# The second query halves turned on VectorE, and two large transfers moved in the first turn

## The reference

```python
q = (x @ Wq.T)                      # 32 heads of 128
q = q * cos + rotate_half(q) * sin  # rotate_half: [-q2, q1], halves of 64
k, v = low-rank keys (part of them rotated too), values   # 8 key/value heads
scores = q @ k.T / sqrt(128), causal; attn = softmax(scores)
x = layernorm(x + (attn @ v) @ Wo.T)
x = layernorm(x + W2(silu(W1 x) * (W3 x)))   # 4-bit weights
```

## Time and profile before

| What | Before |
|---|---|
| median of three runs | 2376.82 us |
| the profiled execution, its span | 2375.78 us, 2374.0 us |
| TensorE matmul busy | 2359.8 us, 99% of the span |
| ScalarE busy | 1619.1 us, 68% |
| VectorE busy | 1425.0 us, 60% |
| GpSimd busy | 577.5 us, 24% |
| chain that ended last | TensorE 96%, DMA 2%, ScalarE 1%, VectorE 1% |
| `b_ys<-y_d`, a load of 256 KB, to landing | 2.7 us |

### The profile page before, as it was taken

The page is one execution under the profiler, slowest core; times in us unless marked ns, Lnnn a source line. Parts: engine busy times, 40 slices in busy tenths (PEclk is TensorE's granted clock), DMA queues, the critical chain, the costliest instruction groups (busy, mean ns, idle before and its releaser), DMA issues.

```text
span 2374.0 us, 40892 instructions
## 1 busy us (share of the span) xinstructions
PE 2359.8 (99%) x11999; PEld 1994.7 (84%) x11999; DVE 1425.0 (60%) x3797; ACT 1619.1 (68%) x3223; POOL 577.5 (24%) x451
## 2 busy tenths in 40 slices
PE   9999999999999999999999999999999999999998
PEld 8888888888888888888888888888888888888887
DVE  5335667676766676666666676767676675243333
ACT  4224878888888888887878888888888885222221
POOL 3102323333232323232323333232323220000000
PEclk9999999999999999999999999999999999999999
DMA  6778534435354444344434445354434435320110
GB/s 224 263 259 276 173 133 143 146 129 166 116 173 126 159 134 145 128 141 150 137 131 138 147 135 173 107 176 131 155 126 145 132 138 199 131 72 36 53 36 18
DMA packets 133256, 338.42 MB, mean 143 GB/s; under 512 B 13344, under 2 KB 30752, under 8 KB 122656
## 3 DMA queue, kind: packets, MB, share of 16 engines
q1 hardware_dynamic: 133200, 337.70, 42.1%
HBM read 230.17 MB, written 109.84 MB: 143 GB/s over the span
## 4 chain that ended last, share of the span: by engine, by line
PE 96%; DMA 2%; ACT 1%; DVE 1%; issue 0%; POOL 0%; SPq 0%; ACTq 0%; DVEq 0%; POOLq 0%
PE b_ps L269 45%; PE b_sps L269 32%; PE b_tps L1658 10%; PE b_tps L1717 3%; PE b_ps L1717 3%; PE b_tps L269 2%; DMA v_d<-a_vs 1%; DMA b_kt<-k_d 0%; DMA b_wraw<-in_wqT 0%; ACT b_sc L1102 0%; ACT b_sc L1108 0%; PE b_tps L1579 0%; PE b_sps L1667 0%; ACT b_pt L1123 0%; DVE b_sc L1330 0%
## 5 line engine op out<-in xcount | busy, mean ns | idle before, releaser
L1348 DVE TENSOR_TENSOR b_pt<-b_tps,b_pt 128x512 fp32r<-128x512 f32 (+3 forms) x768 | 426.4, 555 | 304.5 <-ACT b_pt L1123 300.3
L269 PE MATMUL b_sps<-b_kt,b_qs 128*128 128x512 f32 (+4 forms) x2304 | 496.8, 343 | 1.5 <-DMA b_kt<-k_d 1.1
L1108 ACT ACTIVATE b_sc<-b_sc,b_rinv 128x896 f32<-128x896 f32 (+7 forms) x512 | 396.0, 774 | 105.1 <-DVE b_rinv L1338 98.2
L269 PEld LDWEIGHTS b_sps<-b_kt,b_qs 128*128 128x128 f32 x2304 | 403.5, 188 | 55.9 <-issue 2.5
L1123 ACT ACTIVATE b_pt<-b_tps 128x512 fp32r<-128x512 f32 (+3 forms) x768 | 367.4, 478 | 117.3 <-PE b_tps L1658 115.8
L269 PE MATMUL b_ps<-b_pt,b_vt 128*128 128x512 f32 x1584 | 423.9, 399 | 0.3 <-DVE b_ys L1359 0.3
L1102 ACT ACTIVATE b_sc<-b_sc,b_nmax 128x896 f32<-128x896 f32 (+7 forms) x512 | 395.4, 772 | 38.3 <-DVE b_nmax L1330 34.8
L269 PE MATMUL b_ps<-b_xs,b_wq 128*128 128x512 f32 x1512 | 418.7, 402 | 0.0
L269 PE MATMUL b_ps<-b_wo,b_ot 128*128 128x512 f32 x1536 | 415.6, 403 | 0.0
L1330 DVE CUSTOM_DVE_ANT_0 b_sc<-b_sps,b_mask 128x896 f32<-128x896 f32 (+7 forms) x512 | 386.2, 754 | 18.2 <-PE b_sps L269 18.0
L1658 PE MATMUL b_tps<-b_ident,b_sc 128*128 128x128 f32 x2304 | 349.9, 273 | 4.5 <-ACT b_sc L1108 2.3
(11 more groups left out here) (183 smaller groups left out, 2260.2 us busy)
## 6 DMA issues: line engine op xcount, KB each, us to landing
b_xs<-xs_d SPq DMA_DIRECT2D x32, 2048.0 KB, 9.2
y_d<-b_ys SPq DMA_DIRECT2D x128, 256.0 KB, 3.0
b_ys<-y_d SPq DMA_DIRECT2D x121, 256.0 KB, 2.7
b_wraw<-in_wqT SPq DMA_DIRECT2D x64, 256.0 KB, 2.7
k_d<-a_ks SPq DMA_DIRECT2D x32, 512.0 KB, 4.1
v_d<-a_vs SPq DMA_DIRECT2D x32, 512.0 KB, 3.0
b_kt<-k_d SPq DMA_DIRECT2D x64, 256.0 KB, 4.6
b_vt<-v_d SPq DMA_DIRECT2D x16, 1024.0 KB, 4.8
```

Of the source, the lines that this page charges most:

```text
L269: ins = nc.tensor.matmul(out, *every[n], start=(n == 0), stop=(n == len(every) - 1))
L1108: nc.scalar.activation(sc[:, slot, 0:w], sc[:, slot, 0:w], ACT.Copy, scale=rinv[:, slot:slot + 1])\
L1348: nc.vector.tensor_tensor(pt[:, u, LO, 0:nj, h * P:(h + 1) * P], tps[n % 2][:, 0:nj], pt[:, u, HI, 0:nj, h * P:(h + 1) * P], ALU.subtract) ...
```

## The change

Four things are done.

1. For `q1` VectorE now multiplies the product bank by the sine table itself, in two instructions of 64 partitions that also swap the halves (`turn_q`), just ahead of the cosine multiplication. ScalarE's copies and GpSimd's multiplication of `q1` are gone; `q0` stays as it was.
2. For this the second half of the sine table is loaded with its partition halves swapped: three DMAs where there was one.
3. SP issues the 2 MB store `xs_d<-a_xe` (`a_store_x(END)`) ahead of END's first value store, and no longer in step 6 of the first turn. The copy `y_d<-in_x` of 2304 KB goes from step 13 to step 21 of the first turn.
4. The padding ahead of the loop is changed on ScalarE and VectorE.

```diff
--- before.py
+++ after.py
@@ -821,9 +821,7 @@
                         for p in range(4):
                             sp.wait_ge(a_v_out[p], 16 * (V_USES[p] if p >= 2 else 4) + a_OUT0)
                         load_v(0)
-                    if turn == "first" and step == 6:
-                        a_store_x(END)
-                    if turn == "first" and step == 13:
+                    if turn == "first" and step == 21:
                         sp.dma_start(y_rest, x_rest).then_inc(a_y_out, 16)
                     for _bk, kind, a, g in finished(step, turn, 1):
                         if kind == "q0" and a == 3:
@@ -869,11 +867,14 @@
                 sp.wait_ge(a_k_out[slot], 16 * 2 * 2)
             for n in range(8):
                 if n == 2:
-                    sp.dma_start(sinq[:], sinT).then_inc(tab_in, 16)
+                    sp.dma_start(sinq[:, 0:TB], sinT[:, 0:TB]).then_inc(tab_in, 16)
+                    for half in (0, 64):
+                        sp.dma_start(sinq[64 - half:128 - half, TB:S], sinT[half:half + 64, TB:S]).then_inc(tab_in, 16)
                     sp.dma_start(cosq[:], cosT).then_inc(tab_in, 16)
                 if n == 4:
                     load_k(0)
                 a_store_k(END, n)
+            a_store_x(END)
             for n in range(V_LATE):
                 a_store_v(END, n)
             sp.wait_ge(q_mm, 4)
@@ -962,8 +963,8 @@
                         if kind in ("q0", "q1"):
                             split_q(it + g, int(kind == "q1"), h)
                     for _bk, kind, h, g in finished(step, turn, 1):
-                        if kind in ("q0", "q1"):
-                            times_sin(it + g, int(kind == "q1"), h)
+                        if kind == "q0":
+                            times_sin(it + g, 0, h)
                     if turn != "end" and step in WO_SPLIT:
                         split_wo(it, WO_SPLIT.index(step))
                     if turn in ("first", "loop") and step in WQ_SPLIT:
@@ -980,7 +981,7 @@
             split_wq(0, 3)
             for t in range(2, NBLK):
                 a_rope_lo(t)
-            pool.wait_ge(tab_in, 32)
+            pool.wait_ge(tab_in, 64)
             for h in range(GQ):
                 times_sin(0, 0, h)
             turns(pool, turn_of)
@@ -1062,7 +1063,7 @@
                 a_nope_hi(t)
                 for n in range(8):
                     a_v_hi(t, n, a_bank[(VG + n) % a_RING])
-                    for _ in range(4 if n < 4 else 4):
+                    for _ in range(5 if n < 4 else 4):
                         act.sem_inc(placed, 1)
                 a_rope_hi(t + 1)
 
@@ -1130,8 +1131,8 @@
                 nc.scalar.activation(ot[:, i % 2, HI], banks[bk], ACT.Copy).then_inc(ot_hi, 1)
 
             def take(bk, kind, it, a):
-                if kind in ("q0", "q1"):
-                    swap_q(it, int(kind == "q1"), a, bk)
+                if kind == "q0":
+                    swap_q(it, 0, a, bk)
                 elif kind == "va":
                     a_v_hi(END, a, banks[bk])
                 elif kind == "pv":
@@ -1301,9 +1302,17 @@
                 a_nope_lo(t)
                 for n in range(8):
                     a_v_lo(t, n, a_bank[(VG + n) % a_RING])
-                    for _ in range(3 if n < 4 else 3):
+                    for _ in range(2):
                         dve.sem_inc(placed, 1)
                 a_rope(t + 1)
+
+            def turn_q(it, h, bk):
+
+                n = 8 * it + 4 + h
+                dve.wait_ge(q_mm, n + 1)
+                dve.wait_ge(add_done, n + 1)
+                nc.vector.tensor_tensor(sw[0:64], banks[bk][64:128], sinq[64:128, TB:S], ALU.mult).then_inc(sw_done, 2)
+                nc.vector.tensor_tensor(sw[64:128], banks[bk][0:64], sinq[0:64, TB:S], ALU.mult).then_inc(sin_done, 1)
 
             def cos_q(it, blk, h, bk):
                 n = 8 * it + 4 * blk + h
@@ -1359,6 +1368,8 @@
                 nc.vector.tensor_tensor(ys[:, i % 2], banks[bk], ys[:, i % 2], ALU.add).then_inc(y_added, 1)
 
             def take(bk, kind, it, a):
+                if kind == "q1":
+                    turn_q(it, a, bk)
                 if kind in ("q0", "q1"):
                     cos_q(it, int(kind == "q1"), a, bk)
                 elif kind == "va":
@@ -1536,10 +1547,12 @@
             for n in (2, 3):
                 for m in range(4):
                     a_made_lo(n, m)
+            for _ in range(3):
+                dve.sem_inc(placed, 1)
             for t in range(END):
                 a_block_of(t)
             a_nope_lo(END)
-            dve.wait_ge(tab_in, 32)
+            dve.wait_ge(tab_in, 64)
             dve.wait_ge(masked, 4)
             for h in range(GQ):
                 cos_q(0, 0, h, Q_BANK[h])
```

## The result

The changed kernel takes 2392.1 us, median of six runs (2389.8 to 2392.5), against 2377.2 for the kernel before in six runs, three of which are those of the table ahead of the prediction: ratio 1.0062, 95% interval 1.0051 to 1.0072. It is 15 us slower where 4 us of gain were forecast (2372.8 us, range 2369.6 to 2377.2). The profiled execution took 2392.5 us with a span of 2390.7.

What follows compares the result with a forecast made beforehand. TensorE was taken to bound the kernel, busy 99% of the span. Gains of 2.3 + 1.5 + 0.4 less 0.2 us for the first turn gave 4.0 us: 2376.8 to 2372.8 us, range 2369.6 to 2377.2.

Steps and rivals of the forecast that it cites:

- The 2 MB store and the copy of `y`: First turn: earlier store gains 3.8 us (bounds 0 and 3.8), copy at step 21 gains 0.4 (-0.5 to 0.8).
- stall, clock and the wait for weights: First turn, TensorE: 2.3 us stall near 239 us, 1.5 of lower clock behind it, 0.41 for late query weights, all to go.
- ScalarE and GpSimd lose the part, worth 0: Loop: 76 us less on ScalarE, 83 less on GpSimd; TensorE waits for neither, so gain 0 (bounds 0 and 1).
- VectorE gains it; "1.2 to 1.4 us a head": VectorE's two sine products per `q1` head at 0.6 to 0.69 us each, 77 to 88 us in all.
- So 0.2 to 0.4 us of slack stay, and the loop loses nothing.: Steps 12 and 13: normalising behind the second head's sum ends at 693.7 to 693.9, TensorE wants it at 694.10.
- in step 14 the same addition falls in part on time in which VectorE stood for ScalarE's copies: Step 14 of a loop turn: the added VectorE products partly fill its former waiting time; no loss counted.
- VectorE falls late in the loop: Rival, step 13's sum: if two products take over 1.6 us, up to 14 us slower, 2386.8 us; chance 0.07.
- The loop is fetched again: Rival: VectorE's loop of 368 instructions refetched each turn, 14 x 2.7 = 38 us slower, 2411 us; chance 0.02.

Runs made afterwards that it cites:

- e2: Changed kernel with the two transfers back in their old places, only the sine product's move to VectorE left: 2392.9 us.
- e3: Changed kernel, with GpSimd's split of the fourth `wo` weight held back until the third `q1` head's sum is done: 2378.1 us.
- e7: e3 with ScalarE rounding the last `q1` head before the weights, not behind them, in steps 16 to 23: 2371.8 us.
- e8: e3 with VectorE's sine product as one instruction of 128 partitions, the exchange of halves left out: 2370.7 us.
- e6: Changed kernel, with ScalarE rounding the `q1` head behind normalising and exponentials in steps 3 to 15: 2376.7 us.
- e5: Short separate program, not the kernel: VectorE sums, scalings and products, some beside GpSimd subtractions; a sum started together with GpSimd took 1.80 us.

## Why the prediction was wrong

- *The 2 MB store and the copy of `y`.* Right: stall, clock and the wait for weights went as worked out, and alone the moves gain 4.4 us between profiles. What I missed is that the sine's move alone also shortens the stall by 1.3 us and spares the clock (e2), so that the two gains don't add.
- *ScalarE and GpSimd lose the part, worth 0.* Right in the loop. But "worth 0" overlooked their place: the copies stood ahead of ScalarE's rounding of `wo`, and with them GpSimd's split of it began 0.72 us behind the start of the sum, out of its way.
- *VectorE gains it; "1.2 to 1.4 us a head".* Mis-sized. It is 1.44 to 1.45 us (two times 0.72 to 0.73), since the halves change between the instructions. The rest that hangs on it is 0.3 to 0.5 us a turn, 6.3 and 7.4 us between the medians (e3 against e7 and e8).
- *"So 0.2 to 0.4 us of slack stay, and the loop loses nothing."* The step that failed. I named the second head's sum (step 13) as the tight place, and there it held: the normalising, at 695.96 with 0.60 us, was done 0.20 us before the transposes at 696.76. But I dismissed the next place with "in step 14 the same addition falls in part on time in which VectorE stood for ScalarE's copies". I priced every sum at its 0.67 us of the earlier trace rows. The third head's sum begins 0.37 us into a GpSimd split and takes 1.48 us, 0.8 more; 0.68 us lay free there, and the longer pair had used a part. That is 0.8 us a turn (112.10 against 111.33 and 111.35) and 14 to 15 us in all, the first and the last turn included (e3, e6).
- *The rival "VectorE falls late in the loop"* had the way (ScalarE's queue held by the wait for the sum) and nearly the price (14 us against the 19 between forecast and measurement), but the wrong place and condition: a pair over 1.6 us. A pair of 1.45 was enough with the longer sum. It got 0.07.
- *The loop is fetched again.* It did not come, and that was luck of the padding, with the wrong reason and price: the change's own paddings kept the loop at least four and fewer than eight instructions from the edge, and past it the price is 6 us a branch, not 2.7.

## What to carry to other kernels

When work moves between engines, ask what the old work kept apart. ScalarE's two copies cost it time, but with them a GpSimd split came behind VectorE's sum, though no wait in the program made it so. (That the missing copies and the later sum together brought the split forward is argued from the written order; no run separates the two.) After such a move list each GpSimd instruction that may now run beside a VectorE instruction with two SBUF operands. An engine that runs its instructions in written order makes one late result into several: put what the busiest engine waits for ahead of what may wait, as two rows of ScalarE's order did here for 20 us (2392.1 to 2371.9). And a hardware loop's place in its instruction stream is part of the kernel: after each edit of a long loop, look for instruction packets inside it.

## What the runs showed of the hardware

- A VectorE sum of two SBUF operands that starts beside or behind a GpSimd subtraction ends 0.55 us after GpSimd's end: up to 1.80 us against 0.61 in a row (e5), 1.46 to 1.50 in the changed kernel. With an operand in PSUM: 0.67, undisturbed. A VectorE scaling of one SBUF operand: 0.35 in a row, 1.40 beside GpSimd.
- Successive VectorE products of 64x512 start 0.61 us apart on the same half and 0.72 on changing halves.
- A VectorE loop of 368 instructions ran free with its last branch at record 830 and paid 6 us a branch at 834 and 847, 74 to 77 us in the whole kernel; 3.5 us a turn of it were TensorE's wait, and behind one such wait its granted clock was 0.65 for 4.9 us.
